# Inverse roots as exp(-0.5 ln) on ACT in a decoder layer, and the squares of q and k one step sooner

## The reference

```python
def _l2norm(t):
    n = jnp.sqrt(jnp.sum(t * t, axis=-1, keepdims=True))
    return t / jnp.maximum(n, EPS)               # EPS = 1e-12

q = _l2norm(proj(Wq, bq)); k = _l2norm(proj(Wk, bk)); v = proj(Wv, bv)   # 16 heads of 8
attn = einsum('bhid,bhjd->bhij', q, k) / n ** sigmoid(m)
x = x + (einsum('bhij,bhjd->bhid', attn, v) @ Wo + bo)

# block 2: attention on ctx (32 x 77 x 128), values, keys and query all mapped to
# [exp(z), exp(-z)] per head, softmax of the scores / sqrt(128), then fc_w
x = x + xattn(ctx, ctx, _layernorm(x))

# block 3: top-1 of 16 experts by x @ router_w.T, its output scaled by a sigmoid,
# silu-gated expert (128 wide) plus a shared silu-gated expert (512 wide)
x = x + ffn(_layernorm(x))

def _layernorm(x, eps=1e-5):
    return (x - mean(x)) / sqrt(var(x) + eps)
```

## Time and profile before

| | |
|---|---|
| median of 3 runs | 513.48 us (512.52 to 515.56) |
| the profiled execution, its own time | 517.45 us |
| its span | 515.6 us |
| mean granted TensorE clock | 0.921 |
| busy over the span | PE 429.5 us (83%), DVE 298.8 (58%), ACT 263.1 (51%), POOL 201.7 (39%) |
| phase 1 in the trace | 0 to about 117 us |

### The profile page before, as it was taken

The page is one execution under the profiler, slowest core; times in us unless marked ns, Lnnn a source line. Parts: engine busy times, 40 slices in busy tenths (PEclk is TensorE's granted clock), DMA queues, the critical chain, the costliest instruction groups (busy, mean ns, idle before and its releaser), DMA issues.

```text
span 515.6 us, 10998 instructions
## 1 busy us (share of the span) xinstructions
PE 429.5 (83%) x3804; PEld 322.7 (63%) x3804; DVE 298.8 (58%) x886; ACT 263.1 (51%) x603; POOL 201.7 (39%) x280
## 2 busy tenths in 40 slices
PE   2788888777777389999998999799999998888890
PEld 1466566554444268888888887595566666767650
DVE  4777877632665667787877773725733332444434
ACT  5465555347777417777776777424722222333320
POOL 1322222214886626455552000000377501777730
PEclk9999999987888759999998999857999997999996
DMA  6830000001899967667771000000051103788629
GB/s 207 298 97 1 0 0 1 1 0 53 240 259 278 330 160 189 170 180 181 187 198 44 7 4 5 2 0 0 17 175 52 47 1 83 223 286 273 217 63 294
DMA packets 50353, 62.21 MB, mean 121 GB/s; under 512 B 7316, under 2 KB 46772, under 8 KB 48692
## 3 DMA queue, kind: packets, MB, share of 16 engines
q1 hardware_dynamic: 38528, 37.89, 25.1%
q0 software_dynamic: 4864, 20.43, 14.3%
q10 hardware_dynamic: 6912, 3.25, 2.6%
HBM read 43.68 MB, written 20.73 MB: 125 GB/s over the span
## 4 chain that ended last, share of the span: by engine, by line
PE 54%; DVE 15%; ACT 9%; issue 8%; DMA 7%; SPq 5%; ACTq 1%; POOL 0%; DVEq 0%; POOLq 0%
PE bank L709 6%; PE bank L698 5%; PE bank L1234 5%; PE bank L1235 5%; PE bank L1224 4%; PE bank L671 3%; PE bank L1279 3%; DVE mx L778 2%; PE bank L1218 2%; PE bank L733 2%; PE bank L410 2%; PE bank L434 2%; DMA qparts<-qpart 2%; PE bank L397 2%; ACT t_hT L1159 1%
## 5 line engine op out<-in xcount | busy, mean ns | idle before, releaser
L867 ACT ACTIVATE prob<-bank 77x512 f32<-77x512 f32 x128 | 74.3, 595 | 23.4 <-PE bank L698 23.3
L778 DVE TENSOR_REDUCE mx<-bank 128x5 f32<-128x385 f32 (+1 forms) x96 | 54.9, 576 | 18.7 <-PE bank L671 16.0
L1202 POOL DMA_INDIRECT sorted_in<-h_rows,pos_s x32 | 31.5, 986 | 85.9 <-DVE pos_s L1054 76.5
L1207 POOL DMA_INDIRECT routed<-t_y,t_no x48 | 46.4, 966 | 40.8 <-DVE t_y L1092 31.1
L698 PE MATMUL bank<-qst,kst 99*77 99x128 bf16 x512 | 51.0, 223 | 0.2 <-ACT prob L867 0.2
L698 PEld LDWEIGHTS bank<-qst,kst 99*77 99x77 bf16 x512 | 39.2, 117 | 7.8 <-ACT prob L867 3.9
L377 POOL TENSOR_TENSOR qkv<-qkv,rn 128x256 f32<-128x256 f32 x32 | 19.1, 629 | 63.4 <-DVE rn L296 63.4
L1008 DVE TENSOR_TENSOR act<-bank,s_g 128x512 f32<-128x512 f32 x28 | 19.3, 691 | 42.1 <-ACT s_g L1147 42.0
L671 PE MATMUL bank<-kst,qst 96*128 96x77 bf16 x512 | 36.2, 208 | 7.3 <-DVE mx L778 3.7
L1147 ACT ACTIVATE s_g<-bank 128x512 f32<-128x512 f32 x28 | 16.7, 597 | 48.6 <-PE bank L1235 48.6
L1224 PEld LDWEIGHTS bank<-sd,act 128*128 128x128 f32 x224 | 29.2, 192 | 14.9 <-issue 12.3
(11 more groups left out here) (167 smaller groups left out, 1033.3 us busy)
## 6 DMA issues: line engine op xcount, KB each, us to landing
qst<-qparts POOLq DMA_DIRECT2D x36, 256.0 KB, 3.5
t_w<-in_expert_w SPq DMA_DIRECT2D x48, 192.0 KB
qparts<-qpart SPq DMA_DIRECT2D x16, 384.0 KB, 7.7
kst<-kparts POOLq DMA_DIRECT2D x36, 154.0 KB, 3.9
kparts<-kpart SPq DMA_DIRECT2D x16, 231.0 KB, 7.9
sorted_in<-in_fill SPq DMA_DIRECT2D x1, 3168.0 KB, 13.4
t_row<-sorted_in ACTq DMA_DIRECT2D x48, 66.0 KB
qst<-qparts SPq DMA_DIRECT2D x12, 256.0 KB, 6.5
```

The lines of the kernel that those rows point to most:

```text
L778: v.tensor_reduce(mx[:, b % JA, h0:h1], bank[n % 2][:, 0:(h1 - h0) * KEYS].rearrange("p (h k) -> p h k", k=KEYS), AX.X, ALU.max, negate=Tr ...
L867: a.activation(prob[n % PROBS][:].rearrange("p c t -> p (c t)"), bank[2 + n % 2][0:KEYS], ACT.Exp, scale=SCORE_SCALE).then_inc(s["expd"], 1)
L1202: p.indirect_dma_start(out=sorted_in, out_offset=bass.IndirectOffsetOnAxis(ap=pos[:, b:b + 1].bitcast(U32), axis=0), in_=h_rows[:, b], in_ ...
L1207: p.indirect_dma_start(out=routed, out_offset=bass.IndirectOffsetOnAxis(ap=t_no[r][:].bitcast(U32), axis=0), in_=t_y[r][:], in_offset=None ...
```

## The change

The square root and the reciprocal behind it become two ACT activations, a natural logarithm and an exponential of minus half of it, in phase 1 (both layer norms and the norms of q and k) and in `deviation3`. ACT is told at the start to load one set that holds both. The limit of 1e-12 on the norm becomes one of 1e-24 on the sum of squares, before the logarithm. `sq` of a group is taken at the end of the step in which the group is `front`, no longer at the start of the next step, and waits until `ss` of the group before is made. DVE's `bias` of `back` stands between the second and third of the bias additions L310. Names of semaphores that only change (`std` to `log`) are left out of the diff.

```diff
--- before.py
+++ after.py
@@ -196,6 +196,7 @@
             v.wait_ge(s["inv_ready"], 1)
 
         def act_phase0(a):
+            a.preload_act_table_set("natural_log_exp_and_others")
             a.wait_ge(s["scale_in"], 16)
             a.activation(inv_scale[:, 0:1], m_col[:], ACT.Exp, scale=-1.0).then_inc(s["esc"], 1)
             a.wait_ge(s["esc_dve"], 2)
@@ -270,13 +271,14 @@
                     i = v.bn_aggr(ln_mv[k][:, j], ln_stats[k][:, j])
                 i.then_inc(s[mean], 1)
 
-            def scale_and_bias(g, k, std_s, rstd_s, bias_s):
-
-                v.wait_ge(s[std_s], g + 1)
-                v.reciprocal(ln_rstd[k][:], ln_std[k][:]).then_inc(s[rstd_s], 1)
+            def bias(g, k, rstd_s, bias_s):
                 v.wait_ge(s[rstd_s], g + 1)
                 v.scalar_tensor_tensor(out=ln_bias[k][:], in0=ln_mv[k][:, :, 0], scalar=-1.0, in1=ln_rstd[k][:],
                                        op0=ALU.mult, op1=ALU.mult).then_inc(s[bias_s], 1)
+
+            def add_qkv_bias(g, par, j):
+                v.wait_ge(s["qkvp"], g * JP + (j + 1))
+                v.tensor_tensor(qkv[par][:, j], bank[1 + j][:, 0:3 * D], bqkv[:], ALU.add).then_inc(s["qkv1"], 1)
 
             def step(first, front, middle, back):
                 if first:
@@ -287,13 +289,10 @@
                     g, par, _ = middle
                     v.wait_ge(s["sq1"], g + 1)
                     v.tensor_reduce(ss[:], sq[:].rearrange("p j (h d) -> p (j h) d", d=HD), AX.X, ALU.add).then_inc(s["ss1"], 1)
+                    v.wait_ge(s["ss1"], g + 1)
+                    v.tensor_scalar(ss[:], ss[:], L2_EPS * L2_EPS, None, ALU.max).then_inc(s["nmax1"], 1)
                 if first:
-                    scale_and_bias(first[0], 0, "std1", "rstd1", "bias1")
-                if middle:
-                    v.wait_ge(s["nrm1"], g + 1)
-                    v.tensor_scalar(nrm[:], nrm[:], L2_EPS, None, ALU.max).then_inc(s["nmax1"], 1)
-                    v.wait_ge(s["nmax1"], g + 1)
-                    v.reciprocal(rn[:], nrm[:]).then_inc(s["rn1"], 1)
+                    bias(first[0], 0, "rstd1", "bias1")
                 if back:
                     g, par, _ = back
                     v.wait_ge(s["yp"], g + 1)
@@ -302,12 +301,14 @@
                     v.tensor_tensor(x_g, bank[7][:], x_g, ALU.add).then_inc(s["x1"], 1)
                     wait_on_copy(v, s["x1"], g + 1)
                     statistics(g, 1, "stat2", "mean2")
-                    scale_and_bias(g, 1, "std2", "rstd2", "bias2")
                 if front:
-                    g, par, _ = front
-                    for j in range(JP):
-                        v.wait_ge(s["qkvp"], g * JP + (j + 1))
-                        v.tensor_tensor(qkv[par][:, j], bank[1 + j][:, 0:3 * D], bqkv[:], ALU.add).then_inc(s["qkv1"], 1)
+                    for j in range(JP // 2):
+                        add_qkv_bias(front[0], front[1], j)
+                if back:
+                    bias(back[0], 1, "rstd2", "bias2")
+                if front:
+                    for j in range(JP // 2, JP):
+                        add_qkv_bias(front[0], front[1], j)
                 if middle:
 
                     g, par, _ = middle
@@ -319,9 +320,13 @@
             loop1(v, step, dve_constants)
 
         def act_phase1(a):
-            def deviation(g, k, mean, std_s):
+            def log_variance(g, k, mean, log_s):
                 a.wait_ge(s[mean], g + 1)
-                a.activation(ln_std[k][:], ln_mv[k][:, :, 1], ACT.Sqrt, bias=eps[:]).then_inc(s[std_s], 1)
+                a.activation(ln_std[k][:], ln_mv[k][:, :, 1], ACT.Ln, bias=eps[:]).then_inc(s[log_s], 1)
+
+            def inverse_deviation(g, k, log_s, rstd_s):
+                a.wait_ge(s[log_s], g + 1)
+                a.activation(ln_rstd[k][:], ln_std[k][:], ACT.Exp, scale=-0.5).then_inc(s[rstd_s], 1)
 
             def normalise(g, k, bias_s, dst, done):
                 a.wait_ge(s[bias_s], g + 1)
@@ -330,30 +335,38 @@
                 i.then_inc(s[done], 1)
 
             def step(first, front, middle, back):
-                if middle:
-                    g, par, _ = middle
-                    a.wait_ge(s["qkv1"], g * JP + JP)
-                    a.activation(sq[:], qkv[par][:, :, 0:2 * D], ACT.Square).then_inc(s["sq1"], 1)
                 if front:
                     g, par, _ = front
                     a.wait_ge(s["xT1p"], g + 1)
                     a.copy(xnT[par][:], bank[0][:]).then_inc(s["xT1"], 1)
                 if first:
-                    deviation(first[0], 0, "mean1", "std1")
+                    log_variance(first[0], 0, "mean1", "log1")
                 if middle:
-                    a.wait_ge(s["ss1"], middle[0] + 1)
-                    a.activation(nrm[:], ss[:], ACT.Sqrt).then_inc(s["nrm1"], 1)
+                    a.wait_ge(s["nmax1"], middle[0] + 1)
+                    a.activation(nrm[:], ss[:], ACT.Ln).then_inc(s["nrm1"], 1)
+                if first:
+                    inverse_deviation(first[0], 0, "log1", "rstd1")
+                if middle:
+                    a.wait_ge(s["nrm1"], middle[0] + 1)
+                    a.activation(rn[:], nrm[:], ACT.Exp, scale=-0.5).then_inc(s["rn1"], 1)
                 if first:
                     g, par, _ = first
                     normalise(g, 0, "bias1", xn[par], "xn1")
                 if back:
                     g, par, _ = back
-                    deviation(g, 1, "mean2", "std2")
+                    log_variance(g, 1, "mean2", "log2")
+                    inverse_deviation(g, 1, "log2", "rstd2")
                     normalise(g, 1, "bias2", xn2[par], "xn2")
                 if middle:
                     g = middle[0]
                     a.wait_ge(s["qTp"], g + 1)
                     a.copy(qT[:], bank[5][:]).then_inc(s["qT1"], 1)
+                if front:
+                    g, par, _ = front
+                    a.wait_ge(s["qkv1"], g * JP + JP)
+                    if not is_first(g):
+                        a.wait_ge(s["ss1"], g)
+                    a.activation(sq[:], qkv[par][:, :, 0:2 * D], ACT.Square).then_inc(s["sq1"], 1)
                 if back:
                     g = back[0]
                     a.wait_ge(s["xT2p"], g + 1)
@@ -835,7 +848,7 @@
                     statistics(b - 2)
                 if b >= 3:
                     aggregate(b - 3)
-            inverse_root(v, 0)
+            v.wait_ge(s["rstd3"], 1)
             normalise3(v, 0)
             add_attention(B - 2)
             divide(B - 1)
@@ -850,7 +863,7 @@
             v.memset(onesf[:], 1.0)
             for g in range(2, NG - 1):
                 normalise3(v, g)
-            inverse_root(v, 1)
+            v.wait_ge(s["rstd3"], 2)
             normalise3(v, NG - 1)
 
         def act_phase3(a):
@@ -960,13 +973,9 @@
         def deviation3(a, k):
             lo, hi = NORMED[k]
             a.wait_ge(s["mean3"], hi)
-            a.activation(std[:, lo:hi], mv[:, lo:hi, 1], ACT.Sqrt, bias=eps[:]).then_inc(s["std3"], 1)
-
-        def inverse_root(v, k):
-            lo, hi = NORMED[k]
-            v.wait_ge(s["std3"], k + 1)
-            v.reciprocal(rstd[:, lo:hi], std[:, lo:hi]).then_inc(s["rstd3"], 1)
-            v.wait_ge(s["rstd3"], k + 1)
+            a.activation(std[:, lo:hi], mv[:, lo:hi, 1], ACT.Ln, bias=eps[:]).then_inc(s["log3"], 1)
+            a.wait_ge(s["log3"], k + 1)
+            a.activation(rstd[:, lo:hi], std[:, lo:hi], ACT.Exp, scale=-0.5).then_inc(s["rstd3"], 1)
 
         def normalise3(v, g):
             for j in range(JP):
```

More of the change, by code:

```diff
@@ L139, in decoder_layer @@
                   "ones_rows", "ones_in", "set", "tavp", "rden", "avn", "t2p", "t2", "fcp", "x2", "stat3", "mean3",
-                  "xb2", "std3", "xn3", "h_kept", "hTp", "hT", "lgp", "rstd3", "lg", "r_step", "oh", "rankp",
+                  "xb2", "log3", "xn3", "h_kept", "hTp", "hT", "lgp", "rstd3", "lg", "r_step", "oh", "rankp",
                   "escore", "sc_ready", "pos", "rows", "scat", "etile", "gup", "silu", "act", "downp", "x3", "tTp",
```

## The result

The changed kernel takes 506.85 us (median of 4 runs, 506.3 to 508.68) against 513.73 us of the kernel before on the same chip (4 runs, 512.52 to 515.56): 0.9869 of it, 95% interval 0.9829 to 0.9909, so 6.9 us or 1.3% less. The forecast was 507.3 us. The experiments ran later, in three sets on three chips (4, 12 and 15 in the record), each set beside the kernel before, which takes 566.1, 566.07 and 566.23 us there. In the third set the changed kernel takes 560.46 against 566.23 us, ratio 0.990 (0.9862 to 0.9938).

A forecast was written before the change was run, and what follows sets the result against it. TensorE was taken to bound phase 1's loop, with DVE adding 0.28 us a step. Gains of 1.2 (start), 1.4 (loop) and 3.6 us (pipeline end) sum to 6.2, taking 513.48 to 507.3 us; range 504.2 to 511.4.

The forecast's parts named there:

- What bounds the kernel: Phase 1 loop: TensorE's order is all but closed, asking for 11.85 us of a 12.13 us step; DVE adds 0.28.
- Start, 1.2 us: Start of phase 1: the table load at L324 leaves the path, 1.28 - 0.05 = 1.2 us gained.
- The statement that the weights are no bound: Start: the weights' transfer does not limit the gain as long as DVE's casts of them do not move.
- Loop, 1.4 us: Phase 1 loop: both waits at the end of TensorE's step go, five steps by 0.28 us = 1.4 us.
- End, 3.6 us: End of phase 1's pipeline: TensorE's 1.99 us wait before L417 goes, and 1.6 us of low clock with it.
- Elsewhere nothing: Later phases: table loads at phase 2's start, at 323.98 us and ahead of L1140 are covered; removing them gains nothing.
- the rival in which the other loads count too: The load at 323.98 us also counts: 1.28 us more come off, 506.0 us in all; chance 0.09.
- The last step of phase 1: Statistics, logarithm, exponential and bias in a row, with an exponential for a reciprocal: gains nothing.
- a sum of 6.2: Whole kernel: 1.2 at the start, 1.4 in the loop and 3.6 at the pipeline's end make 6.2 us gained.
- The port rival: Phase 1 loop: POOL gets the port before DVE's bias of first; 512.3 us in all; chance 0.06.
- lost to all four: In the port rival, DVE's bias waits out all four of POOL's L377, 0.63 us each, 2.5 us.

The follow-up runs named there:

- stream_2: Changed kernel with two instead of three of the products nobody reads behind L433 in phase 1; 0.9807 of the kernel before.
- both load experiments: preload, on the kernel before, 0.9989 of its time; load_again, on the changed kernel, 0.9876 of the kernel before.
- the second pair: Second traces of the kernel before and the changed kernel, both unmodified, on different chips; the changed kernel's ratio there is 0.9900.
- load_again: Changed kernel with exp_and_others loaded first and the logarithm's table set loaded right ahead of the first logarithm; 0.9876 of the kernel before.
- pool_first: Changed kernel with the exponential for rn ahead of the one for ln_rstd of first on ACT; 0.9879 of the kernel before.
- preload: Kernel before with the square root's table set loaded right after the two first exponentials, where ACT is idle; 0.9989 of the kernel before.
- sq_late: Changed kernel with only the squares back at their old place, at the start of the step of middle; 0.9902 of the kernel before.

## Why the prediction was right

**What bounds the kernel: right.** It put the step at 11.85 us for TensorE and 0.28 for DVE's delay. The step came out at 11.82, and `stream_2` shows directly that it is TensorE's now, by giving back a product's own time.

**Start, 1.2 us: right at its place, 0.8 us at the mark.** The first long product starts 1.23 us earlier, and both load experiments repeat it (1.27 and 1.18 us). At the first mark the first pair of traces has 0.81 us, since the eight products took 4.88 instead of 4.46 us, and the second pair 2.06 us, since they took 4.54 instead of 5.37. The statement that the weights are no bound held: DVE waits until 9.26 us for them in the changed kernel, off the path. The 2.66 us for a switch that the Trainium skill states (ScalarE: Activation LUTs, What ACT_TABLE_LOAD costs) does not show here: 1.28 us is all, with ACT idle ahead of the load (the change, `load_again`) and with ACT busy ahead of it (the load at 323.98 us).

**Loop, 1.4 us: 1.6 measured** (5 x 0.31), from the exponential in place of the reciprocal. The addition to `x` came 66.15 - 64.64 = 1.51 us behind the start of the q, k, v products and comes 63.46 - 62.88 = 0.58 us behind it now, 0.93 us sooner where 0.9 was forecast. `xn2` was said to be 1.0 us ahead of TensorE; it is 1.1.

**End, 3.6 us: 3.63 measured,** by the squares chiefly, with the clock at 1.00; 4.06 in the second pair. The split into 1.99 us of wait and 1.6 of clock holds: from the mark before to L417 (L430) it was 102.75 - 96.51 = 6.24 us and is 98.12 - 94.04 = 4.08, 2.16 less, and from there to the last mark 5.51 and now 4.04 us, 1.47 less. In the second pair the clock's part is 1.90 us.

**Elsewhere nothing: right for the loads.** The change itself took the other three away, and the places show what that brought. Around the one at 323.98 us, before and changed:

```profile
323.52 0.71 PE L733 MATMUL bank<-fcw,avnT 128*128 128x128 f32 x4
...
316.19 0.71 PE L746 MATMUL bank<-fcw,avnT 128*128 128x128 f32 x4
...
318.18 0.44 PE L740 MATMUL bank<-first_pack,avn_s 128*128 128x128 f32 x2 [0.28 <-DVE avn_s L816]
```

From the one product to the next TensorE took 325.50 - 323.52 = 1.98 us with the load between on ACT and takes 318.18 - 316.19 = 1.99 us without. At phase 2's start `kf` comes 1.90 us behind the start of ACT's copy `ctxT_s` in both, and the exponential of phase 4 comes 0.73 us behind the start of DVE's `best` in both. So the rival in which the other loads count too falls. The last step of phase 1 was not quite nothing: the low clock at its last turn costs 0.45 us in both traces of the changed kernel. The last marks are 6.10 us apart against a sum of 6.2, but 7.78 us in the second pair (2.06 + 1.57 + 0.09 + 4.06). Behind them the traces scatter by 5 us without regard to the kernel. So the terms are right, and that the median came within 0.5 us of the forecast is in part luck.

**The port rival: wrongly priced.** The prediction had DVE locked out through all four of L377, 2.5 us, and 512.3 us in all. `pool_first` made it happen: 0.60 us, and no time lost. The step that failed is "lost to all four": the port is free between two instructions. The rule itself (the Trainium skill, SBUF — State Buffer, Who interferes with whom: a DVE instruction with two SBUF inputs contends with a GpSimd one that reads SBUF, and the shared ports are an exclusive lock) agrees with the row, for one instruction.

## What to carry to other kernels

Find the engine whose order is closed, measure what it asks for in a step where nothing is late, and take the difference as all that a faster neighbour can bring: here 0.3 us a step although a whole 0.95 us reciprocal left DVE. Look at the steps where a software pipeline runs out as a case of their own: they have the longest uncovered chains, and moving one activation across a step boundary brought more there than all the loop's savings. When the neighbours have been made fast enough, work that only keeps the closed engine busy is the next thing to take away.

## What the runs showed of the hardware that I had not expected

- The port shared by DVE and POOL changes hands between two POOL instructions: a bias that came 0.05 us behind POOL took 0.60 us instead of 0.16, not 2.39.
- An activation that waits for the one ahead of it on ACT costs next to nothing: the exponential at 5.79 us starts 0.03 us after the logarithm's end.
- A table load costs its 1.28 us and nothing more, even right behind another activation: 0.01 us ahead of it and 0.02 behind it at 323.98 us.
- TensorE's first eight long products of the program take 4.3 to 5.5 us, the next eight 2.85, with the granted clock recorded as 1.00 for both; the first ones run at the pace of 0.50, and when they become fast is the largest scatter ahead of the first mark.
- A wait of 1.99 or 2.00 us ahead of the last L417 was followed by slow matmuls in both traces of before and in `preload`, one of 1.35 us in `sq_late` was not.
